# Scaling factors of the last layer written into PSUM, where VectorE reads them

## The reference, cut to what matters

```python
agg = jax.ops.segment_sum(x[src], dst, num_segments=N_NODES)
h = agg @ W.T
h = jax.nn.relu(h)
h = h + h_in
...
x = _layernorm(x + _L3_gnn_ref(x, src, dst, L3_gnn_W), axis=-1)
```

## Time and profile before

| | us |
|---|---|
| median of 3 runs | 3239.19 (3236.39 to 3239.74) |
| span of the profiled execution, first to last instruction | 3236.0 |
| the last layer within it, from its first gather to the end | 2679.5 to 3236.0 |
| VectorE busy, share of the whole span | 2647.0, 82% |
| POOL busy, share of the whole span | 1871.0, 58% |

### The profile page before, as it was taken

One profiled execution on the slowest core, in us unless ns is written; L12 is line 12 of the kernel. 1 busy time (PEld: TensorE's weight loads), 2 busy tenths in 40 slices (PEclk: granted clock), 3 DMA queues, 4 the chain that ended last, 5 costly groups with the idle time before them and its releaser, 6 DMA issues. The chain is left out here.

```text
span 3236.0 us, 46376 instructions
## 1 busy us (share of the span) xinstructions
PE 2560.1 (79%) x14129; PEld 1752.9 (54%) x14129; DVE 2647.0 (82%) x3328; ACT 2099.4 (65%) x3677; POOL 1871.0 (58%) x1771
## 2 busy tenths in 40 slices
PE   7899999959999977888888699999999752345500
PEld 3466666636666655566665456766666541234400
DVE  6599999969999987999999457888888756999910
ACT  0167776736566557999988588989989753545500
POOL 4477777523333327777775555555555006787776
PEclk9999999979999998999999899999999855666855
DMA  7357666656666656777776448878887547885211
GB/s 210 111 186 226 218 219 221 209 164 199 198 197 200 202 153 204 234 234 232 229 229 210 117 132 201 210 202 214 205 213 201 147 120 247 276 273 155 83 39 40
DMA packets 495088, 611.79 MB, mean 189 GB/s; under 512 B 66866, under 2 KB 284652, under 8 KB 494717
## 3 DMA queue, kind: packets, MB, share of 16 engines
q1 hardware_dynamic: 433030, 495.63, 50.9%
q0 software_dynamic: 56480, 111.88, 13.0%
q10 hardware_dynamic: 5334, 1.32, 0.2%
HBM read 391.94 MB, written 220.55 MB: 189 GB/s over the span
## 5 line engine op out<-in xcount | busy, mean ns | idle before, releaser
L1295 POOL DMA_INDIRECT g_xd_xs<-table_x,dst_row x196 | 200.7, 1024 | 285.1 <-PE g_psT L1363 191.1
L1817 POOL DMA_INDIRECT f_rows<-table_x,src_row x196 | 228.0, 1163 | 229.0 <-POOLq L1216 169.6
L775 POOL DMA_INDIRECT c_xs<-table_x,src_row x196 | 185.0, 944 | 303.0 <-PE c_psT L916 249.8
L765 POOL DMA_INDIRECT c_xs<-table_h,src_row x196 | 221.4, 1130 | 121.4 <-issue 78.9
L497 POOL DMA_INDIRECT xs<-in_x,src_i x196 | 227.2, 1159 | 85.4 <-issue 55.5
L482 POOL DMA_INDIRECT xd<-in_x,dst_i x196 | 216.4, 1104 | 94.8 <-issue 47.2
L1295 POOL DMA_INDIRECT g_xd_xs<-table_x,src_row x196 | 208.3, 1063 | 59.8 <-issue 59.8
L1824 POOL DMA_INDIRECT out<-f_rows,end_i x196 | 197.5, 1008 | 62.4 <-issue 62.4
L1869 PE MATMUL f_psT<-w_ident,f_rows 128*128 128x128 f32 x196 | 48.6, 394 | 220.8 <-DVE f_rows L1962 220.8
L765 POOL DMA_INDIRECT c_xd<-table_h,dst_row x196 | 185.0, 944 | 59.7 <-issue 59.7
L1368 PEld LDWEIGHTS g_psP<-w_center,g_turns 128*128 128x128 f32 x1568 | 183.7, 191 | 49.9 <-ACT g_turns L1504 28.4
(11 more groups left out here) (332 smaller groups left out, 8595.0 us busy)
## 6 DMA issues: line engine op xcount, KB each, us to landing
g_share<-shares SPq DMA_DIRECT2D x196, 192.0 KB
xn<-in_x SPq DMA_DIRECT2D x49, 512.0 KB
table_x<-xo SPq DMA_DIRECT2D x49, 512.0 KB, 2.9
table_x1b<-xb SPq DMA_DIRECT2D x49, 512.0 KB, 4.9
c_xn<-table_x SPq DMA_DIRECT2D x49, 512.0 KB
table_h<-c_xo SPq DMA_DIRECT2D x49, 512.0 KB
c_xn<-table_h SPq DMA_DIRECT2D x49, 512.0 KB
c_x1r<-table_x1b SPq DMA_DIRECT2D x49, 512.0 KB
```

Source lines behind the costliest of these rows:

```text
L765: pool.indirect_dma_start(out=quarters(rows[:, s, :])[j], out_offset=None, in_=table, in_offset=edge_index(columns, now.n, j)).then_inc(la ...
L775: pool.indirect_dma_start(out=quarters(xs[:, s, :])[j], out_offset=None, in_=table, in_offset=edge_index(h.src_row, now.n, j)).then_inc(sr ...
L1295: pool.indirect_dma_start(out=quarters(xd_xs[:, s, k, :])[j], out_offset=None, in_=table, in_offset=edge_index(columns, now.n, j)).then_in ...
L1817: pool.indirect_dma_start(out=quarters(rows[:, n, :])[j], out_offset=None, in_=table, in_offset=edge_index(h.src_row, n, j)).then_inc(src_ ...
```

## The change

The factors `rstdn` and `rstde` become views of two PSUM banks that nothing else used, `node_factors` and `edge_factors`. ScalarE's two `Exp` (L1907, L1915) write there, and VectorE's scalings L1962, L1964 and L1970 read their second input from there. `rstd`, the second factors of the edge rows, which L1980 reads, stays in SBUF. No instruction, wait or transfer is added or removed, and the order of all engines is as it was.

```diff
-        varn, lnvn, rstdn = (sb(n, [P, 16]) for n in ("varn", "lnvn", "rstdn"))
-        sqe, vare, lnve, rstde = sb("sqe", [P, 2, TILE]), sb("vare", [P, 8]), sb("lnve", [P, 8]), sb("rstde", [P, 8])
+        varn, lnvn = (sb(n, [P, 16]) for n in ("varn", "lnvn"))
+        sqe, vare, lnve = sb("sqe", [P, 2, TILE]), sb("vare", [P, 8]), sb("lnve", [P, 8])
...
         psT, psY, psE = ([bank(f"{n}{k}") for k in range(2)] for n in ("psT", "psY", "psE"))
+        node_factors, edge_factors = bank("node_factors"), bank("edge_factors")
+        rstdn, rstde = node_factors[:, 0:16], edge_factors[:, 0:8]
```

## The result

The changed kernel took 3219.07 us (median of 4 runs, 3217.51 to 3221.5) against 3238.35 us for the kernel before beside it (3236.39 to 3239.74): a ratio of 0.9943, 95% interval 0.9931 to 0.9956, so 19.3 us less. The forecast was 3223 us, 16 less, in a range from 3217 to 3229.5. A second measurement of the same kernel later gave 0.9945 (0.9929 to 0.9962).

A forecast was written before the change was run, and what follows sets the result against it. POOL's 196 gathers then 196 scatters in the last layer were taken to bound the kernel. -16.7 (store wait takes over) + 0.4 (scatters) + 0 (PSUM) = -16.3 us, from 3239.2 to 3223 us; range 3217 to 3229.5.

The forecast's parts named there:

- the likeliest case: Last layer: the wait for the node-row stores takes over after shorter gathers; 3220 to 3226 us, chance 71%.
- scatters without a hold: Rival: with three holders fewer in a step, scatters fall into none of L1980; 5.4 us more off, 3217.5 us, 5%.
- The hold: Gathers beside L1962, L1964, L1970 no longer held, only L1980 holds; last gather starts at 2931.5 us, 34.5 us earlier.
- What is late next: Between gathers and scatters POOL waits for the last node-row store; first scatter at 2950.5 against 2967.2 us, -16.7 us.
- Store to first scatter: After the last node-row store's issue at 2946.3: 3.5 us landing plus 0.7 us release, first scatter at 2950.5 us.
- The scatters: One holder a step, L1980, is enough to keep their loss; beside 23 instead of 21 steps it grows by 0.4 us.
- The PSUM side: ScalarE's Exp writing PSUM and VectorE's scalings reading it: taken as 0, Exp bounded by ±0.9 us over 24 steps.
- Slower through the queues: Rival: more gathers a pair step tip the DMA queues over, pair loads come late, VectorE's steps stretch; 3%.
- A slower VectorE: Rival: each of three scalings pays 0.067 us for reading PSUM, last store 5.0 us later; 3228 us, 12%.
- no change: Rival: the hold has another reason than the second SBUF input, gathers still end at 2966; 3239 us, 8%.
- two larger gains: Rivals: the whole loss comes back, 3205 us, 1%; or scatters fall into none of L1980, 3217.5 us, 5%.
- The whole loss: Rival: nothing waits for the stores, so scatters start at 2932.8 us; 3205 us, 1%.

## Why the prediction was right

*The number.* 3219.07 us lies 0.9 us below the range of the likeliest case, 3220 to 3226, and inside the stated range because that was stretched down to 3217 for scatters without a hold, which did not come about. So the mechanism was right and the whole range held by some luck: several small terms, below, all fell on the same side.

*The hold.* Right, and shown: the long instruction made to read one SBUF tensor gives the gain, the two others alone give 4 us of it, and taking the last holder away from the scatters frees them too. Forecast for the gathers was 252 us from first to last start, measured 250.7. L1982 first met a gather in its third step, not its first. By the rule of the Trainium skill's page "SBUF — State Buffer", section "Who interferes with whom", that a VectorE instruction with two SBUF inputs contends with a GpSimd instruction that reads SBUF, the traces agree; by its inference that `tensor_tensor` does not stall the making of descriptors they do not: a gather takes 2.50 us beside the long `tensor_tensor` with two SBUF inputs, and 0.94 us beside the same one with its factors in PSUM.

*What is late next.* Right: a 17.7 us wait where 18 was forecast, and the two kernels with two pairs less, one 14.8 and the other 2.2 us faster, show that it gates only behind the change. Store to first scatter was put at 4.2 us and measured 3.7.

*The scatters.* Right that one holder is enough and that L1982 keeps the loss up, though before it was L1964 that held most of them, which the prediction did not say. The sign of the small term was wrong: +0.4 forecast, -0.5 measured (258.2 us), since VectorE's step became shorter and a scatter is put back by the difference of step and four intervals, 5.31 - 5.15 = 0.16 instead of 0.20 us.

*The PSUM side.* This term was mis-sized. I took nothing, with a bound of ±0.9 us for `Exp`. The write saves 0.029 us an `Exp`, and VectorE's wait for it in a pair step went from 0.69 to 0.66 us. VectorE's steps are 0.04 us shorter, with and without a pair, so the last pair's scaling starts 1.2 us earlier, counted from the first gather (264.4 against 265.6), more than the 0.9 us of the bound. The edge rows' factors alone do it: with only the node rows' factors in PSUM the steps stay at 10.48 and 5.35 us and that scaling at 265.7, with only the edge rows' they are 10.44 and 5.31 us and it starts at 264.3. In a step without a pair the first scaling starts 1.19 us behind the scan (2956.82 less 2955.63) where it was 1.22. The profile lists no wait for `Exp` there, but before, `Exp` ended at 2955.67 and the scaling started at 2955.70, the same 0.03 us behind it as in a pair step; now `Exp` ends ahead of that point, at 2956.78, and the scan sets the start. So `Exp` had been last by a hair in these steps too. The Trainium skill's page "ScalarE: Activation LUTs", in the step-by-step section, has a write to PSUM as faster than one to SBUF; the 0.180 against 0.209 us agree. The larger fixed cost of a PSUM source that the Trainium skill's page "VectorE: DVE Perf Modes" gives in the section on the errata does not show with one of two inputs in PSUM: 0.686 us against 0.692.

*The sum.* In the layer: -1.2 by the pair steps, -0.5 by the landing, -0.5 by the scatters, and -16.7 that stood in the forecast for the end of the hold: -18.9 us, against -16.3 forecast. The medians give -19.3. Of the 3.9 us between 3223 and 3219.07, 2.6 lie in the layer and 0.8 in the median of the kernel before, 3238.35 where the forecast had 3239.19.

*The rivals.* Slower through the queues did not happen: the DMA share in the pair steps rose from 0.89 to 0.91 and the loads of pairs land in 6.8 instead of 6.5 us in the median, far from the 14 that would cost. A slower VectorE and no change are refuted by the rows above. Of the two larger gains, the one by the scatters did not come, since L1982 still holds them; the prediction priced it at 3217.5, and with that holder taken away it is 3215.0. The whole loss came back only with the edge work later, which is another kernel.

## What to carry to other kernels

Where GpSimd issues indirect DMAs beside VectorE, look at the longest of their instructions, not at the mean: a few at 2.5 us among many at 0.94 point to VectorE instructions with two SBUF inputs, and here it was enough to move the small operand of the longest one to PSUM. When two engines run in periods, the loss is what the period leaves over after a whole number of the other's instructions, so removing some of several holders can bring next to nothing (4 us here), and removing the longest nearly all. And before counting on a shorter stretch, find the wait that its slack had hidden: here that wait took 17.7 of 36 us, and reordering the work that it waits for gave them back, 13 with four steps and the rest with six.

## What the runs showed of the hardware that had not been expected

In these traces a POOL gather is held at one point only, about 0.12 us after its start: if a VectorE instruction with two SBUF inputs runs then, the gather ends 0.82 us after that instruction does (a scatter 0.86), and one that starts later does not touch it. With that one rule and VectorE's times of the trace, the last gather of the kernel before comes out at 2964.7 (measured 2966.0), and its last scatter, counted from the first one and with the 2.75 us gap put in, at 3225.9 (measured 3225.9).

Of the three holders in a row in a pair step, one short and one long each put back a gather; with the short ones gone, the long one alone costs the same (1.71 against 1.74 us a step). ScalarE's `Exp` of 8 columns is 0.029 us shorter into PSUM than into SBUF.
